# Soft experts: the first layer's bias added on VectorE, and the next group's first layer moved between a group's transposes and its second layer

## The reference

```python
h = gelu(einsum('bnpd,ndh->bnph', xs, w1) + b1)      # 64 experts, 8 rows each, 192 -> 768
ys = einsum('bnph,nhd->bnpd', h, w2) + b2            # 768 -> 192
```

## Time and profile before

| | |
|---|---|
| Runs | 2396.60, 2398.55, 2399.64 us; median 2398.55 us |
| Profiled execution, its span | 2403.1 us, 4.55 us above the median of the runs |
| Busy TensorE / VectorE / ScalarE / GpSimd | 1879.3 / 1495.5 / 1074.7 / 395.9 us |
| Mean granted TensorE clock | 0.834 of full speed |

### The profile page before, as it was taken

How to read it: one execution, slowest core, us unless ns; L and a number is a source line. 1 busy time by engine, 2 the same in 40 slices (tenths; PEclk the granted TensorE clock), 3 DMA queues, 4 the chain that set the end, 5 groups by cost and what they waited for, 6 DMA issues and landing times. The chain is left out here.

```text
span 2403.1 us, 30974 instructions
## 1 busy us (share of the span) xinstructions
PE 1879.3 (78%) x9780; PEld 1007.5 (42%) x9804; DVE 1495.5 (62%) x2518; ACT 1074.7 (45%) x1896; POOL 395.9 (16%) x595
## 2 busy tenths in 40 slices
PE   3868788858876453777668877998899984999994
PEld 2745655535333320000022234442133333888883
DVE  4558449966010687999878876999788883111114
ACT  1100222214110476999979964342477661222220
POOL 5000000000112010222100003331033343222221
PEclk8989999968887575555589978997799996999997
DMA  3011110005797004443011008777666703566664
GB/s 85 1 39 31 48 31 27 20 10 229 309 411 314 20 0 127 127 127 123 18 32 40 26 16 119 130 132 107 83 88 95 97 28 135 195 201 203 202 203 184
DMA packets 147792, 264.98 MB, mean 110 GB/s; under 512 B 28864, under 2 KB 115985, under 8 KB 142678
## 3 DMA queue, kind: packets, MB, share of 16 engines
q1 hardware_dynamic: 135750, 242.10, 38.0%
q0 software_dynamic: 10768, 18.19, 2.3%
q10 hardware_dynamic: 1152, 3.15, 0.3%
HBM read 221.85 MB, written 57.71 MB: 116 GB/s over the span
## 5 line engine op out<-in xcount | busy, mean ns | idle before, releaser
L1743 PE MATMUL ps<-arena 128*128 x376 | 194.9, 621 | 108.2 <-ACT ps L1785 60.1
L1785 ACT ACTIVATE ps<-ps,arena 128x512 f32<-128x512 f32 x384 | 256.7, 1121 | 6.3 <-POOL arena L1769 6.3
L1753 DVE TENSOR_REDUCE arena<-ps 128x1024 f32 x192 | 232.8, 1225 | 24.5 <-PE ps L1743 12.2
L1785 ACT ACTIVATION_READ_ACCUMULATOR ps<-ps,arena 128x1 f32 x384 | 234.7, 668 | 0.0
L2159 DVE TENSOR_REDUCE arena<-ps 128x1024 f32 x192 | 221.3, 1219 | 12.4 <-PE ps L2405 9.8
L2618 ACT ACTIVATE arena<-ps 128x1024 f32<-128x1024 f32 x192 | 185.1, 1020 | 97.6 <-PE ps L2500 96.4
L2962 DVE TENSOR_TENSOR arena<-ps,arena 128x384 f32<-128x384 f32 x39 | 21.8, 558 | 286.4 <-PE ps L2918 286.4
L2942 ACT ACTIVATE arena<-ps,arena 128x256 f32<-128x256 f32 x234 | 89.5, 481 | 235.9 <-PE ps L2907 230.0
L2405 PE MATMUL ps<-arena 96*128 96x512 bf16 x500 | 162.7, 430 | 26.4 <-DVE arena L2159 12.2
L1950 ACT ACTIVATE arena<-ps 128x1024 f32<-128x1024 f32 x192 | 178.7, 1048 | 7.8 <-DVE arena L1970 4.6
L529 PE MATMUL ps<-arena 96*128 96x456 f32 (+1 forms) x512 | 170.3, 482 | 8.8 <-DMA arena<-la_xt 5.2
(11 more groups left out here) (394 smaller groups left out, 3264.8 us busy)
## 6 DMA issues: line engine op xcount, KB each, us to landing
arena<-in_sm_w_dram SPq DMA_DIRECT2D x128, 576.0 KB, 15.5
arena<-in_re_w_dram SPq DMA_DIRECT2D x39, 1252.0 KB, 5.9
arena<-ra_parts SPq DMA_DIRECT2D x192, 192.0 KB, 9.1
routed_in<-routed_in SPq DMA_DIRECT2D x8, 3332.0 KB, 14.2
ra_parts<-arena SPq DMA_DIRECT2D x48, 192.0 KB, 2.4
arena<-routed_in SPq DMA_DIRECT2D x39, 196.0 KB, 5.4
arena<-la_xt SPq DMA_DIRECT2D x16, 384.0 KB, 3.4
arena<-arena SPq DMA_DIRECT2D x64, 96.0 KB, 2.2
```

The source lines that it names most:

```text
L1743: ins = pe.matmul(ps[:, 2 * (n % 4) + t % 2, :], QM[j][:, h, t * P:(t + 1) * P], KI[:, b, h // HG, :], start=True, stop=True)
L1753: v.tensor_reduce(MXq[:, b, 2 * u:2 * u + 2, at_head(h)], ps[:, 2 * (n % 4):2 * (n % 4) + 2, :], AX.X, ALU.max).then_inc(s_lk, 1)
L1785: ins = act.activation(bank, bank, ACT.Exp, bias=nb[n % 4][:, t % 2:t % 2 + 1], scale=c_reg, accum_out=RS[:, b, t, at_head(h):at_head(h) + 1])
```

## The change

VectorE now adds the bias: `bias(g)` adds the first layer's sums in PSUM and a bias tile in SBUF and writes `HG`; the gelu works on `HG` in place. TensorE's bias matmuls and `pick` are gone. The bias tile has 128 partitions: for each expert, a transfer of its own copies the bias row to the eight used partitions of its quarter. GpSimd zeroes the three tiles ahead of that, and SP's first loads wait for it. `out` is cut in two, `turn(g)` (transposes) and `out(g)` (second layer), and hidden(g+1) stands between them. SP waits for the bias addition (`hb`) where it waited for hidden (`hp`).

```diff
     for q in range(GE):
         sp.dma_start(m.EW[:, GE * r + q, w], io.sm_w[GE * g + q][:, w]).then_inc(done, 16)
-    if part == 0:
-        sp.dma_start(B1[r], io.sm_b1[GE * g:GE * g + GE, :]).then_inc(done, 16)
+        if part == 0:
+            sp.dma_start(B1[r][32 * q:32 * q + B], io.sm_b1[GE * g + q].partition_broadcast(B)).then_inc(done, 16)
...
             for g in range(RING):
+                sp.wait_ge(s_bz, g + 1)
                 for part in range(2):
                     ring_load(sp, m, io, B1, g, part)
...
-            pool.memset(pick, 0.0).then_inc(s_pick, 1)
...
+            for r in range(RING):
+                pool.memset(B1[r], 0.0).then_inc(s_bz, 1)
...
+            def bias(g):
+                hp.wait(v, g, 1)
+                tp.wait(v, g, -1)
+                v.tensor_tensor(HG[g % 2].rearrange("p (a h) -> p a h", a=2), ps[:, 2 * (g % 2):2 * (g % 2) + 2, 0:HH],
+                                B1[g % RING].rearrange("p (a h) -> p a h", a=2), ALU.add).then_inc(hb.sem, 1)
+
             stage(0)
             stage(1)
+            bias(0)
             for g in range(NGR):
...
                 v.tensor_copy(HT[j].rearrange("p (a k) q -> p a (k q)", a=2),
                               ps[:, 4:6, 0:3 * P]).then_inc(tc.sem, 1)
+                if g + 1 < NGR:
+                    bias(g + 1)
...
-                hp.wait(act, g, 1)
-                tp.wait(act, g, -1)
-                act.activation(HG[j].rearrange("p (a h) -> p a h", a=2),
-                               ps[:, 2 * j:2 * j + 2, 0:HH], ACT.Gelu).then_inc(gl.sem, 1)
+                hb.wait(act, g, 1)
+                act.activation(HG[j], HG[j], ACT.Gelu).then_inc(gl.sem, 1)
...
-                gl.wait(pe, g, -1)
+                hb.wait(pe, g, -1)
                 for half in range(2):
-                    pe.matmul(ps[:, 2 * j + half, 0:HH], pick.rearrange("p g c -> p (g c)"),
-                              B1[g % RING][:, half * HH:(half + 1) * HH], start=True, stop=False)
...
             hidden(0)
             for g in range(NGR):
+                turn(g)
                 if g + 1 < NGR:
                     hidden(g + 1)
                 out(g)
...
                 if g == RING:
-                    hp.wait(sp, g - RING, 1)
+                    hb.wait(sp, g - RING, 1)
                     ring_load(sp, m, io, B1, g, 0)
                 if g + 1 < NGR:
-                    hp.wait(sp, g + 1 - RING, 1)
+                    hb.wait(sp, g + 1 - RING, 1)
                     ring_load(sp, m, io, B1, g + 1, 0)
```

More of the change, by code:

```diff
@@ L941, in ring_load @@
         sp.dma_start(m.EW[:, GE * r + q, w], io.sm_w[GE * g + q][:, w]).then_inc(done, 16)
-    if part == 0:
-        sp.dma_start(B1[r], io.sm_b1[GE * g:GE * g + GE, :]).then_inc(done, 16)
-FIRST_LOAD, RING_LOAD = 16 * (GE + 1), 16 * GE
+        if part == 0:
+            sp.dma_start(B1[r][32 * q:32 * q + B], io.sm_b1[GE * g + q].partition_broadcast(B)).then_inc(done, 16)
+FIRST_LOAD, RING_LOAD = 2 * 16 * GE, 16 * GE
 def soft_moe(nc, m, io):
@@ L960, in soft_moe @@
     phi, phisq = g3(DC, [NC, NE]), g3(DC, [NC, NE])
-    ones, pick = g3(DC, [DC]), g3(GE, [GE, 32])
+    ones = g3(DC, [DC])
     XSs = [g3(P, [2, GE, 32]), g1(P, [2, GE, 32])]
-    B1 = [g2(GE, [HID]) for _ in range(RING)]
+    B1 = [g2(P, [HID]) for _ in range(RING)]
     mt, rt, cm, cs = two(NE, [1]), two(NE, [1]), two(P, [T]), two(P, [T])
@@ L1032, in soft_moe @@
         "combine_turned", "combine_stored", "slots", "slots_stored"))
-    s_pick = sem("sm_bias_rows_picked")
+    s_bz = sem("sm_bias_rows_zeroed")
     mx, ex, ce, s_lk = S1("slot_max"), S1("dispatch_exp"), S1("combine_exp"), sem("sm_chain")
@@ L1192, in _ @@
         def _(pool):
-            pool.memset(pick, 0.0).then_inc(s_pick, 1)
[L1194 to L1197, removed]
+            for r in range(RING):
+                pool.memset(B1[r], 0.0).then_inc(s_bz, 1)
     NGR = NE // GE
-    st, hp, gl, tp, tc, yp, yc = (Signal(nc, f"sm_{n}", 1, 2) for n in (
-        "slots_staged", "hidden", "gelu", "hidden_turned", "hidden_turned_copied", "expert_out", "out_copied"))
+    st, hp, hb, gl, tp, tc, yp, yc = (Signal(nc, f"sm_{n}", 1, 2) for n in (
+        "slots_staged", "hidden", "hidden_biased", "gelu", "hidden_turned", "hidden_turned_copied", "expert_out",
+        "out_copied"))
     s_y = [nc.alloc_semaphore(f"sm_out_stored{j}") for j in range(2)]
@@ L1210, in _ @@
             st.start(v)
+            hb.start(v)
             tc.start(v)
@@ L1215, in stage @@
                 v.tensor_copy(XSs[g % 2][:, :, :, 0:B], XS[:, :, GE * g:GE * g + GE, :]).then_inc(st.sem, 1)
+            def bias(g):
[3 more added lines that the diff above has]
+                                B1[g % RING].rearrange("p (a h) -> p a h", a=2), ALU.add).then_inc(hb.sem, 1)
             stage(0)
             stage(1)
+            bias(0)
             for g in range(NGR):
                 j = g % 2
-                if g > 0 and g + 1 < NGR:
+                if g and g + 1 < NGR:
                     stage(g + 1)
@@ L1256, in hidden @@
                 pe.wait_ge(m.ring_first[g % RING], FIRST_LOAD * (g // RING + 1))
-                gl.wait(pe, g, -1)
+                hb.wait(pe, g, -1)
                 for half in range(2):
-                    pe.matmul(ps[:, 2 * j + half, 0:HH], pick.rearrange("p g c -> p (g c)"),
-                              B1[g % RING][:, half * HH:(half + 1) * HH], start=True, stop=False)
                     for q in range(GE):
                         pe.matmul(ps[32 * q:32 * q + 32, 2 * j + half, 0:HH], XSs[j][:, 0, q, :],
-                                  m.EW[:, slot + q, half * HH:(half + 1) * HH], start=False, stop=False)
+                                  m.EW[:, slot + q, half * HH:(half + 1) * HH], start=True, stop=False)
                 for q in range(GE):
@@ L1269, in hidden, with turn @@
                 ins.then_inc(hp.sem, 1)
-            def out(g):
-                j, slot = g % 2, g % RING * GE
+            def turn(g):
                 gl.wait(pe, g, 1)
@@ L1276, in out @@
                     ins = pe.transpose(ps[:, 4 + k // 3, k % 3 * P:(k % 3 + 1) * P],
-                                       HG[j].rearrange("p (q k) -> p k q", k=KH)[:, k, :], m.ident)
+                                       HG[g % 2].rearrange("p (q k) -> p k q", k=KH)[:, k, :], m.ident)
                 ins.then_inc(tp.sem, 1)
+            def out(g):
+                j, slot = g % 2, g % RING * GE
                 tc.wait(pe, g, 1)
```

## The result

The changed kernel takes 2410.53 us (median of 7 runs, 2408.22 to 2419.37) against 2397.16 for the kernel before (7 runs). The ratio is 1.0066, 95% interval 1.0047 to 1.0086: slower, where no measurable change was forecast, and outside the stated range. (The quotient of the two medians is 1.0056, inside the interval.) The profiled execution took 2409.97 us, so its time is its span of 2408.0 plus 2 us.

A forecast was written before the change was run, and what follows sets the result against it. The weight stream was taken to pace the expert groups. Start -1.6, load +4.4 and tail -1.7 summed to +1.1 us, on 2398.55 giving 2399.7 us, with a range of 2394.5 to 2404.5.

The forecast's parts named there:

- What bounds the stage: Expert groups: from about 620 us the weight stream sets the pace, 11.82 us a group; TensorE matters only at the ends.
- The start: From hidden(0) to the ring's first new loads: without bias matmuls the stream resumes earlier, -1.6 us.
- the bound of -2.1: Stream's start: the term's faster limit, -2.1 us, if TensorE's clock has risen before hidden(1).
- The stream's load: Weight stream, groups 4 to 15: added bias bytes on eight engines cost 0.37 us a group, +4.4 us.
- The tail: After part 0 of group 15 lands: new order shortens what remains by 0.8 to 2.6 us, taken as -1.7.
- the wait ahead of out(14): Stage's end: group 14's second layer waits for its part 1, landing 5.9 us after group 15's part 0; previously hidden.
- The hidden costs: Memsets delay first loads 0.8 us and SP issues 1.4 us more a group; both were expected to be hidden.
- Rival 2: Weight stream: bias rows cost more than their bytes, eight engines reading the same memory; twice gives +5.6 us; chance 0.13.

The follow-up runs named there:

- e1: Changed kernel without any transfer of bias rows, so its result lacks the bias; ratio 0.9978 to the kernel before.
- e2: Kernel before with the changed kernel's four eight-row bias transfers a group added, to partitions nothing reads; ratio 1.0092 to the kernel before.
- e6: Changed kernel with an expert's eight rows on every fourth partition instead of neighbouring ones, staging copy and output stores included; ratio 1.0020 to the kernel before.
- e3: Changed kernel with eight different bias table rows as each transfer's source instead of one row eight times; ratio 1.0058 to the kernel before.
- e7: Changed kernel with each bias transfer cut to the first 48 of 768 columns, 192 bytes a row; ratio 0.9992 to the kernel before.
- e9: Kernel before with all bias rows loaded once ahead of the groups, old order and bias matmuls kept; ratio 1.0036 to the kernel before.
- e8: Kernel before with the new TensorE order and all bias rows loaded once ahead of the groups, bias matmuls kept; median 2400.55 us, ratio 1.0009.
- e4: Kernel before with only the new TensorE order (transposes, next group's first layer, second layer), bias matmuls and four-row transfer kept; ratio 0.9998 to the kernel before.
- e10: The same kernel as e8, run and profiled again without an edit; median 2400.41 us, ratio 1.0020 to the kernel before.
- e14: A single further profiled execution of e8's kernel, without an edit; 2405.20 us, no ratio.

## Why the prediction was wrong

**What bounds the stage: right.** The stream paced it in every kernel, and 26 us less of busy TensorE was worth nothing between the stage's ends.

**The start: right in mechanism, too small.** A lead of 2.1 us was forecast for the first issue and 1.6 for the second; counted from the stage's start they were 2.3 and 3.2, and hidden(1) ended 4.2 us earlier. The lead grew because TensorE's clock rose before hidden(1) was through (its second half took 0.88 us where hidden(0)'s took 1.53); the bound of -2.1 for that case priced it too low.

**The stream's load: the step that failed.** "Twelve groups (4 to 15) lie behind the point where the stream resumes: 12 x 0.37 = +4.4 us". It measured +15.5 (139.3 to 154.8), 1.3 us a group. The step priced the transfers as if only the engines that carry them were held up, and for their bytes. The runs show two things in its place, both of which the bias transfers bring (e1, e2). The weight transfers beside them slow down: 191 ns a packet instead of 181, 390 GB/s at an unchanged share. And the engine that comes last falls further behind the mean, some 0.6 us a group.

Worked out per group against e1, which has no bias transfers (13.05 - 11.53 = 1.5 us): an estimate of 0.24 us for the 98.3 KB at the mean rate and 0.6 for the slower weight packets (10 ns x 1,024 packets / 16 engines) make up the rate's share of 0.9; 0.6 is the lag of the last engine, of which the bytes of four rows on each of eight engines explain about 0.24 (0.49 for these engines, by the rate used in the forecast, less the 0.24 of the mean). So the bytes account for some 0.5 us of 1.5, 6 of 18 us over twelve groups. Another 6 to 7 us go with neighbouring destinations (e6); the transfers' source (e3) and their number (e7) are not it. The remaining 5 us or so go with the bytes as well (e7) and have no mechanism that the runs separate. Nor do they show what it is in a neighbouring destination that costs, or why it is 15% of the weight packets that take so long.

**The tail: the mechanism right, the size not shown.** -1.7 was forecast, 16.6 to 14.9 measured, with the wait ahead of out(14) in the trace (3.20 us). The number agrees by luck, though: the second profile of before has 13.9, and against that it is no gain.

**The hidden costs:** the memsets and the longer issue on SP cost nothing visible (the changed kernel's stage begins at 603.8 and 601.2, before's at 604.4 and 603.2).

**Rival 2 was the one that came,** with a chance of 0.13, in its direction and not by its reason. Its threshold was 0.68 us a group, its highest price 0.74; 1.3 was measured. The parts of the stage add up to -4.2 + 15.5 - 1.7 = +9.6 us in the stage, where the forecast had +1.1. The range ended at a doubling of the bytes' price, with no row of the trace to bound it. The kernel before could not have given it away: its own four-row transfer costs (139.3 - 137.9) / 12 = 0.12 us a group by e9 in the old order and (139.5 - 137.4) / 12 = 0.18 by e8 against e4 in the new one, close to its bytes' price of 0.12.

**Open** is why kernels with the bias loaded once have medians at (e8, e10) or above (e9) before although their stream is 2 us shorter. e7 does something like it: its stage was 162.8 us, its ratio 0.9992, and its stage began at 607.8. In the kernels with the bias loaded once the stage begins at 605.1 to 608.4 in five of seven profiles and at 598.8 and 600.3 in those of e10 and e8; over all kernels here it begins anywhere from 598.1 to 608.4, with code ahead of it that the edits hardly touch. Most of the difference between e8 and e10 and the three later profiles of the same kernel lies in this start and in the clock behind it. Whether these kernels meet a late and cold start more often than before, or so many profiles fell that way, the runs don't tell.

## What to carry to other kernels

Where a stream of weights paces a stage, work taken from a compute engine is worth nothing between the stage's ends, and what is put into that stream in its place has to be paid, here at several times its bytes. Replicated rows, eight times the bytes of the plain ones, cost 1.3 us of an 11.8 us group, although they were 2% of its bytes. Left with TensorE, which waits for landings anyway, the work costs nothing there; fetched once ahead of time the rows gave the shortest stream, but no faster program than before. And before a shorter stage in one profile is believed, compare its clock windows and where its stage begins with those of a second profile: here 7 us came and went with the clock at the stage's start.

## What was unexpected of the hardware

Eight-row transfers of 3,072 bytes a row lowered the rate of the whole queue from 410 to about 370 GB/s while they passed, at an unchanged DMA share of 1.02 to 1.03: weight packets beside them took 191 ns instead of 181. They also spread the engines: at the end of the stream some were done 11 us ahead of the last, where the rate before falls from full to nearly nothing within 4 us. The same rows on every fourth partition cost 6 to 7 us less over twelve groups (e6), and the same transfers with 192 bytes a row almost nothing (e7). The same kernel starts the stage at a granted clock of 1.00 or 0.50 from one execution to the next (e10 and e14), and its start takes 10.2 or 17.6 us.
